# A new order of work on ScalarE, VectorE and GpSimd in the attention steps of a fused transformer block

## What is computed

```python
x = x + L0_xattn(layernorm(x), ctx)          # one head
x = x + L0_ffn(layernorm(x))                 # dense, with a routed low-rank part
# third block: 32 query heads, 8 key/value heads of 128
q = rmsnorm(heads(layernorm(x) @ q_proj.T), q_norm_w)
k = rmsnorm(heads(ctx @ k_proj.T), k_norm_w);  v = heads(ctx @ v_proj.T)
scores = q @ k.T / sqrt(128) + mask          # four query heads share one k and v
x = x + (softmax(scores) @ v) @ o_proj.T
x = x + down(silu(gate(n)) * up(n))          # n = layernorm(x), 4-bit weights
```

## Time and profile before

| | us |
|---|---|
| median of 3 runs (lowest, highest) | 960.37 (960.29, 961.23) |
| profiled execution: time | 960.64 |
| its span (first to last instruction) | 958.8 |
| outside the span | 1.8 |

### The profile page before, as it was taken

The page is one execution under the profiler, slowest core; times in us unless marked ns, Lnnn a source line. Parts: engine busy times, 40 slices in busy tenths (PEclk is TensorE's granted clock), DMA queues, the critical chain, the costliest instruction groups (busy, mean ns, idle before and its releaser), DMA issues.

```text
span 958.8 us, 14594 instructions
## 1 busy us (share of the span) xinstructions
PE 888.9 (93%) x4096; PEld 709.9 (74%) x4096; DVE 601.8 (63%) x1132; ACT 462.7 (48%) x1716; POOL 513.3 (54%) x559
## 2 busy tenths in 40 slices
PE   6999999979699999999999899999986899999996
PEld 5786887867487777777777777777765678888885
DVE  6316514323466666666666666666665579899887
ACT  4543740324455555555555555555563244443442
POOL 4333450322766666666666666666655246556562
PEclk9999999989899999999999999999997999999999
DMA  7401010112555555645555555565762224443312
GB/s 254 161 30 56 23 54 13 45 34 77 167 173 167 169 166 165 177 150 168 168 168 168 155 168 168 169 170 161 227 207 77 88 77 154 153 153 141 125 41 89
DMA packets 75249, 126.46 MB, mean 132 GB/s; under 512 B 8429, under 2 KB 46061, under 8 KB 75182
## 3 DMA queue, kind: packets, MB, share of 16 engines
q1 hardware_dynamic: 75182, 125.74, 42.0%
HBM read 90.06 MB, written 35.65 MB: 131 GB/s over the span
## 4 chain that ended last, share of the span: by engine, by line
PE 41%; DVE 23%; ACT 17%; issue 11%; POOL 5%; DMA 2%; ACTq 1%; DVEq 1%; SPq 0%; POOLq 0%
PE bank L1211 9%; PE bank L1212 8%; PE bank L1213 8%; ACT prob L765 7%; DVE bank L1053 6%; DVE split L1018 4%; DVE nmax L1059 4%; DVE tb L1045 4%; ACT headT L736 3%; ACT probT_hi L727 3%; PE bank L1379 3%; ACT aoT_hi L741 3%; PE bank L1380 3%; PE bank L1408 2%; PE bank L1409 2%
## 5 line engine op out<-in xcount | busy, mean ns | idle before, releaser
L765 ACT ACTIVATE prob<-bank,nmax 128x128 f32<-128x128 f32 x256 | 90.7, 366 | 84.2 <-DVE nmax L1059 84.2
L756 ACT ACTIVATE bank<-bank 128x128 f32<-128x128 f32 x256 | 67.9, 265 | 130.2 <-DVE tb L1040 130.2
L1211 PE MATMUL bank<-split,xnT_hi 128*128 128x512 f32 x288 | 115.6, 401 | 4.8 <-POOL split L464 4.8
L1212 PE MATMUL bank<-split,xnT_hi 128*128 128x512 f32 x288 | 113.3, 393 | 0.0
L1213 PE MATMUL bank<-split,xnT_lo 128*128 128x512 f32 x288 | 113.2, 393 | 0.0
L1211 PE MATMUL bank<-split,aoT_hi 128*128 128x512 f32 x256 | 103.0, 402 | 3.9 <-DVE aoT_lo L1032 3.9
L1032 DVE TENSOR_TENSOR aoT_lo<-bank,aoT_hi 128x512 fp32r<-128x512 f32 x64 | 44.3, 692 | 96.3 <-ACT aoT_hi L741 96.3
L1438 PEld LDWEIGHTS bank<-kv,headT 128*128 128x128 f32 x512 | 63.8, 195 | 52.5 <-issue 34.9
L1212 PE MATMUL bank<-split,aoT_hi 128*128 128x512 f32 x256 | 102.0, 398 | 0.0
L1213 PE MATMUL bank<-split,aoT_lo 128*128 128x512 f32 x256 | 101.9, 398 | 0.0
L1438 PE MATMUL bank<-kv,headT 128*128 (+1 forms) x512 | 75.0, 291 | 27.8 <-ACT headT L736 27.4
(11 more groups left out here) (151 smaller groups left out, 2210.2 us busy)
## 6 DMA issues: line engine op xcount, KB each, us to landing
block_bounce<-tb SPq DMA_DIRECT2D x244, 128.0 KB, 2.3
land<-block_bounce SPq DMA_DIRECT2D x61, 512.0 KB, 3.2
raw<-in_wqo_dram SPq DMA_DIRECT2D x62, 256.0 KB, 3.0
kv<-in_ffn_w_dram SPq DMA_DIRECT2D x14, 768.0 KB, 4.4
kv<-in_ffn_z_dram SPq DMA_DIRECT2D x14, 768.0 KB, 5.6
kv<-in_up_s_dram SPq DMA_DIRECT2D x14, 256.0 KB, 5.9
resid<-in_x_dram SPq DMA_DIRECT2D x2, 1024.0 KB, 8.8
kv<-in_ctx_dram SPq DMA_DIRECT2D x1, 2048.0 KB, 10.6
```

Of the source, the lines that this page charges most:

```text
L756: done = act.activation(bank[5][:, tile(h)], bank[i % 2][:, tile(h)], ACT.Square, accum_out=ssq[:, i % 2, h:h + 1])
L765: done = act.activation(prob[:, tile(h)], bank[2 + i % 2][:, tile(h)], ACT.Exp, bias=nmax[:, h:h + 1], accum_out=rsum[:, h:h + 1])
L1211: pe.matmul(dst, l_hi, r_hi, start=first, stop=False)
L1212: pe.matmul(dst, l_hi, r_lo, start=False, stop=False)
```

## The change

What moves, by engine, in `step(j)`:

- **ACT.** Before: probT_hi(j+1), headT(j+4), aoT_hi(j), squares(j+6), exponentials(j+4), vcur_hi(j+2). After: squares(j+5), weight_hi of chunk j+10, headT(j+5), aoT_hi(j+1), probT_hi(j+2), exponentials(j+4), vcur_hi(j+2).
- **DVE.** `weight_hi` leaves it. Before: add_out(j-1), rinv(j+3), aoT_lo(j), weight_hi, tb of queries j+6, tb of prob j+3, mask and maximum(j+4). After: rinv(j+3), add_out(j-1), tb of prob j+3, tb of queries j+6, mask and maximum(j+4), aoT_lo(j+1).
- **POOL.** Before: probT_lo(j+1), prob(j+3), weight_lo, rms(j+6), vcur_lo(j+2). After: prob(j+3), vcur_lo(j+1), rms(j+5), weight_lo, probT_lo(j+2).
- **Buffers.** `land` has two slots and `tb` one (before, the other way round). `bounce_read` now waits for copies one step older; the two transposes of a step wait for the bounce write of the step before.
- **SP.** A weight chunk is issued behind the bounce write of its step, not ahead of the read; chunks 4 to 9 come one step later (`EARLY_CHUNKS`), and so do their rounding and rest. Chunk 10 is issued in step 0 (before, step -1).
- **Start.** The first query weights are rounded one to three places earlier; `values(10)` is made ahead of Q(0), and V11 to V15 in steps -6 to -2, one a step.
- **End.** `ln_lo(3, 0..3)` on DVE and `ln_hi(3, 0..3)` on ACT move into step 61; the first gate product moves ahead of O(62).

```diff
-        tb = sb("tb", [P, 2, 2 * D])
-        land = sb("land", [P, 2 * D])
+        tb = sb("tb", [P, 2 * D])
+        land = sb("land", [P, 2, 2 * D])
...
-        VALUES_AT = {-6: (10, 11), -5: (12, 13), -4: (14,), -3: (15,)}
+        VALUES_AT = {-6: (11,), -5: (12,), -4: (13,), -3: (14,), -2: (15,)}
+        EARLY_CHUNKS = {-2: (4, 5), -1: (6, 7), 0: (8, 9)}
...
 # SP, bounce_read(c)
-                if c >= 1:
-                    sp.wait_ge(s_qt, min(c, STEPS))
-                if c >= PLAG + 1:
-                    sp.wait_ge(s_ptl, c - PLAG)
+                if c >= 2:
+                    sp.wait_ge(s_qt, min(c - 1, STEPS))
+                if c >= PLAG + 2:
+                    sp.wait_ge(s_ptl, c - PLAG - 1)
...
 # POOL, step(j)
+                if valid(j + 3):
+                    i = j + 3
+                    pool.wait_ge(s_ri, at(p, i) + 1)
+                    pool.tensor_tensor(heads(prob[:]), heads(prob[:]), over(rinv[:, 0:REP], P), ALU.mult)\
+                        .then_inc(s_pn, 1)
                 if valid(j + 1):
                     i = j + 1
...
+                    g = i // T if p is None else 2 * p + i // T
+                    pool.wait_ge(s_vh, at(p, i) + 1)
+                    pool.tensor_tensor(vcur_lo[:], val[:, bass.ds(g * P + (i % T) * NKV * P, P)], as32(vcur_hi[:]),
+                                       ALU.subtract).then_inc(s_vl, 1)
...
 # ACT, ahead of the steps
-            for m in range(T + 2):
+            for m in range(T + 3):
                 copy_values(m)
                 if 3 <= m:
                     ln_hi(2, m - 3)
-                if T <= m:
-                    hi(WGRP + m - T)
-            ln_hi(2, T - 1)
-            for c in range(WGRP + 2, WGRP + KT):
-                hi(c)
+                for c in ((WGRP, WGRP + 1), (WGRP + 2,), (WGRP + 3,))[m - T + 1] if T - 1 <= m < T + 2 else ():
+                    hi(c)
...
 # ACT, step(j), behind the squares and headT
+                if p is not None or 0 <= j < STEPS - 10:
+                    weight_hi(10 + j, p)
...
+                if valid(j + 1):
+                    act.wait_ge(s_e, at(p, j + 1) + 1)
+                    if p is not None or j >= 0:
+                        act.wait_ge(s_f, at(p, j + 1))
+                    act.activation(aoT_hi[:], bank[6][:], ACT.Copy).then_inc(s_ah, 1)
+                if valid(j + 2):
+                    i = j + 2
+                    act.wait_ge(s_br, 16 * (at(p, i) + PLAG + 1))
+                    if p is not None or i >= 1:
+                        act.wait_ge(s_e, at(p, i))
+                    act.activation(by_head(probT_hi[:]), landed(i + PLAG, 1), ACT.Copy).then_inc(s_pt, 1)
...
 # DVE, step(j)
+                if p is None and j == STEPS - 3:
+                    for t in range(HALF):
+                        ln_lo(3, t)
+                if valid(j + 1):
+                    dve.wait_ge(s_ah, at(p, j + 1) + 1)
+                    dve.tensor_tensor(aoT_lo[:], bank[6][:], as32(aoT_hi[:]), ALU.subtract).then_inc(s_al, 1)
```

More of the change, by code:

```diff
@@ L758, in step @@
                     done.then_inc(s_sq, 1)
+                for m in VALUES_AT.get(j, ()) if p is None else ():
+                    copy_values(m)
+                for n in EARLY_CHUNKS.get(j, ()) if p is None else ():
+                    weight_hi(n, None)
+                if p is not None or 0 <= j < STEPS - 10:
+                    weight_hi(10 + j, p)
+                if valid(j + LEAD - 1):
+                    i = j + LEAD - 1
+                    act.wait_ge(s_br, 16 * (at(p, i) + 1))
+                    if p is not None or i >= 1:
+                        act.wait_ge(s_c, at(p, i))
+                    act.activation(by_head(headT[:]), landed(i, 0), ACT.Copy).then_inc(s_qt, 1)
+                if p is None and j == STEPS - 3:
+                    for t in range(HALF):
+                        ln_hi(3, t)
+                if valid(j + 1):
[6 more added lines that the diff above has]
+                    act.wait_ge(s_br, 16 * (at(p, i) + PLAG + 1))
+                    if p is not None or i >= 1:
+                        act.wait_ge(s_e, at(p, i))
+                    act.activation(by_head(probT_hi[:]), landed(i + PLAG, 1), ACT.Copy).then_inc(s_pt, 1)
                 if valid(j + 4):
@@ L1029, in step @@
                     dve.reciprocal(rinv[:, 0:REP], rsum[:, 0:REP]).then_inc(s_ri, 1)
-                if valid(j):
-                    dve.wait_ge(s_ah, at(p, j) + 1)
-                    dve.tensor_tensor(aoT_lo[:], bank[6][:], as32(aoT_hi[:]), ALU.subtract).then_inc(s_al, 1)
-                if p is not None or 0 <= j < STEPS - 10:
-                    weight_hi(10 + j, p)
+                if valid(j - 1):
+                    add_out(j - 1, p)
+                if valid(j + 3):
+                    i = j + 3
+                    dve.wait_ge(s_pn, at(p, i) + 1)
+                    dve.wait_ge(s_bw, 16 * KT * (at(p, i) + PLAG))
+                    dve.transpose(blocks_of(1), split32(prob[:])).then_inc(s_tp, 1)
                 if valid(j + LEAD):
@@ L1114, in _ @@
                 if j == STEPS - 2:
-                    for t in range(HALF):
-                        ln_lo(3, t)
                     ln_aggr(3, HALF, HALF + 2)
@@ L1429, in step @@
                     done.then_inc(s_a, 1)
+                for m in VALUES_AT.get(j, ()) if p is None and j < -2 else ():
+                    values(m)
                 if valid(j + 4):
@@ L1458, in step @@
                     attend()
+                if p is None and j == STEPS - 2:
+                    pe.wait_ge(s_ex, STEPS)
+                    gate(0, None, 0)
                 if p is None and j == STEPS - 1:
```

136 lines of the change are left out of this document (44 added, 92 removed).

## The result

The changed kernel takes 986.35 us (median of 4 runs, 984.8 to 987.76) against 960.33 us for the kernel before (4 runs, 959.63 to 961.23): a ratio of 1.027, 95% interval 1.0252 to 1.0288. I had forecast 972, 962 to 982. The direction was right, the change is over twice as large as forecast (26.0 us for 11.7), and the time lies outside the range. The profiled execution has a span of 985.1 us.

A forecast was written before the change was run, and what follows sets the result against it. It took a ring through ACT and DVE, 7.85 us a step, to bound the kernel before, not PE. Stretch terms -14.3 + 4.6 + 10.8 + 4.8 + 6.0 = +11.9 on a median of 960.37 gave 972 us, range 962 to 982.

The forecast's parts named there:

- The ring of the loop: Each attention step: aoT_hi, probT_hi, exponentials, rinv, prob, vcur_lo, E, O wait in turn; 8.08 us, 0.22 longer than before.
- The rule that I weighed: Loop: frequent small PE idle times move the clock, losing more than the ring says; forecast kept the clock at 1.00.
- The loop's edges: Two back edges between O(4) and O(53): some 3.7 us together before, taken as unchanged; bounds 1.3 to 2.6 each.
- item 4: O(4) to O(53), before 388.8 us: 49 steps each 0.22 longer, +10.8.
- The start: Start to O(4): Q(0) at 204.5 as before, Q(0) to O(0) -14.3, O(0) to O(4) +4.6 us.
- Item 2: Q(0) to O(0), before 58.2 us: full clock and fewer waits give 43.9, so -14.3; bound -5.3.
- The two waits before E: Before O(0): E(0) and E(1) wait for exponentials, rinv, prob, vcur_lo; 2.8 us each.
- The stall in step 0: O(0) to O(4): ACT waits for weight chunk 10 until 253.4, headT behind it; +3 us.
- Items 5 and 6: O(53) to O(60): seven steps of 8.08 plus appended work, +4.8 us; O(60) to O(63): later O(61), +6, bounds +2 to +8.
- a rival at 6%: Loop: E and O at 1.2 GHz add some 3.2 us to one step in ten, +18, 990 us; chance 6%.
- O(63) to the end: After O(63): nothing changes.
- The range: Whole kernel: 962 to 982 us, from steps -7 to +7, end -4 to +2, start -3 to +9, edges -1 to +2.

The follow-up runs named there:

- experiments 1 and 2: Changed kernel with POOL's vcur_lo ahead of prob: 933.55 us; with that and ACT's vcur_hi ahead of the exponentials: 921.24 us.
- experiment 6: Changed kernel with weight chunk 10 rounded at the end of step 0 on ACT and POOL: 985.14 us.
- experiments but 4: 4 is the kernel before with only the rounding of weights (weight_hi) moved from DVE to ACT, ahead of the squares: 928.67 us.
- experiment 3: Changed kernel with three unread query products on PE in steps 58 to 60: 983.44 us.
- experiment 8: Experiment 5 with unread query products on PE in steps 58 to 61: 967.35 us.
- experiment 5: Changed kernel with the last steps' extra work moved: DVE's between the maximum and aoT_lo, POOL's ahead of probT_lo: 974.98 us.
- experiment 7: Changed kernel with vcur_hi and vcur_lo moved ahead, the last steps' extra work beside the ring, and chunk 10 rounded at the end of step 0: 904.8 us.
- experiment 11: Experiment 7 with the first two feed-forward units' transfers issued two each behind steps 53 to 55: 905.18 us.

## Why the forecast was right and wrong

**The ring of the loop: right.** I took 8.08 for a step of 8.10; its parts stand in the rows in the order given, and experiments 1 and 2 take it apart one member at a time (7.23, 7.03). The clock stayed at 1.00 over all 49 steps, with the wait of PE before each E. That it would was less sure than I wrote: I gave PE a gap of 0.8 us a step before, from 7.86 - 7.02, but the earlier trace rows have 18.7 us idle in 49 steps, 0.38 a step. The rule that I weighed, from the Trainium skill ("TensorE: Matmul & The Clock Gate", "A second HAM failure mode: psum-queue depth-cycling"), that frequent small idle times let the clock go up and down, is not borne out by this loop: one idle time of 0.84 in 8.10 us left it up.

**The loop's edges: mis-sized by 3.1.** I let the two edges cost what they cost before, some 3.7 together. They cost 0.6: the steps there are 8.41 and 8.35. DVE's late start fell into its wait for the exponentials entirely (rinv waits 1.31 instead of 1.23 there), not for a part of it. The 3.1 saved, less 1.0 for the 0.02 more a step, is the 2.1 by which item 4 came out shorter.

**The start: right in kind, 3.7 longer than forecast.** Q(0) to O(0) fell by 12.4 of the 14.3 forecast. Item 2 took Q(0) at full clock, since the wait ahead of it is short. The wait was 1.90 us, and PE in the changed kernel reads

```profile
204.79 0.50 PE L1203 MATMUL bank<-split,xnT_hi 128*128 128x512 f32 x1 [1.90 <-DVE xnT_lo L907]
...
205.83 0.39 PE L1204 MATMUL bank<-split,xnT_hi 128*128 128x512 f32 x1
206.06 0.58 PE L1205 MATMUL bank<-split,xnT_lo 128*128 128x512 f32 x1
...
242.03 0.47 PE L1203 MATMUL bank<-probT_hi,vcur_hi 128*128 128x512 f32 x1 [1.80 <-POOL vcur_lo L557]
249.77 0.47 PE L1203 MATMUL bank<-probT_hi,vcur_hi 128*128 128x512 f32 x1 [3.03 <-POOL vcur_lo L557]
```

It began at the high level and fell to the low one 1.3 us later, in the midst of work: Q(0) took 4.2 us instead of 2.7. But this was the luck of the profiled execution. In experiment 6, with the same code up to here and the same wait, PE reads

```profile
204.99 0.50 PE L1207 MATMUL bank<-split,xnT_hi 128*128 128x512 f32 x1 [1.90 <-DVE xnT_lo L911]
...
206.25 0.39 PE L1209 MATMUL bank<-split,xnT_lo 128*128 128x512 f32 x1
```

and Q(0) takes 2.9 us. Of the twelve profiles with the new start (the changed kernel and all experiments but 4), all with a wait of 1.90 us, Q(0) stayed at the high level in six and fell in six. Where it stayed, with nothing else changed up to O(0) (experiments 3, 6 and 8), Q(0) to O(0) took 44.2, 43.6 and 43.9 us, my 43.9; where it fell (the changed kernel and experiment 5), 45.8 and 45.3. So item 2 was right but for the clock, which it counted as certain. The two waits before E are 1.80 and 3.03 where I had placed 2.8 each. The stall in step 0 was forecast at 3 us, at its right place, ACT's rounding of chunk 10:

```profile
255.58 0.63 ACT L725 ACTIVATE split<-raw 128x512 fp32r<-128x512 f32 x1 [5.30 <-DMA raw<-in_wqo_dram]
```

It ended 2.2 us later than I had put it (253.4), but so did O(0), which began at 250.6 where I had 248.4; against O(0) the stall was as forecast. The first step was 11.83, not 11.2, and the next two 8.97 and 8.38, not 8.08. Experiment 6, which moves that instruction, has 36.0 us for O(0) to O(4), 1.2 to 2.5 less than the profiles without that edit; the rest of the excess is not taken apart.

**The last ten steps: this is the step that failed.** Items 5 and 6 said 90.1 us; it is 100.2. They took the whole stretch at full clock, and they priced the appended work at its length before. What the runs put in their place:

- *Work of DVE and POOL on the ring*, forecast at 4.8 + 6.0 = 10.8: experiment 5, which takes most of it away, gives 6.3 + 3.1 = 9.4. As a sum that was near; within it a term was far off. For step 57 I had 0.7 on DVE and the clock untouched. With stretch and clock together that step was 3.3 longer than one of the loop. I priced the subtractions by their rows before, about 0.68, and didn't ask what POOL does at that moment. The groups of DVE from 700 to 780 us, of the kernel before and then of the changed one:

```profile
L1080 DVE TENSOR_TENSOR split<-kv 128x512 fp32r<-128x512 int32 x4 | 2.7, 683 | 0.0
```

```profile
L1074 DVE TENSOR_TENSOR split<-kv 128x512 fp32r<-128x512 int32 x3 | 4.1, 1398 | 0.0
L1069 DVE TENSOR_TENSOR kv<-kv 128x512 f32<-128x512 int32 x2 | 3.6, 1778 | 0.0
```

  And two of them one behind the other in the changed kernel, with what POOL does (it is idle behind this):

```profile
736.89 1.76 DVE L1069 TENSOR_TENSOR kv<-kv 128x512 f32<-128x512 int32 x1
738.57 0.68 DVE L1074 TENSOR_TENSOR split<-kv 128x512 fp32r<-128x512 int32 x1
...
736.84 1.26 POOL L575 TENSOR_TENSOR probT_lo<-land,probT_hi 128x512 fp32r<-128x512 f32 x1 [6.67 <-ACT probT_hi L766]
```

  The same instructions take 0.68 when POOL has no such work, here, before and in experiment 5, and some 1.77 where a two-input subtraction or product of POOL (`probT_lo`, `up_scale`) runs at the same time. The rows look as if the two took turns: DVE ends 0.55 behind the end of POOL's instruction, here (738.65 and 738.10) as in step 57 (726.71 and 726.16), and there POOL's product, which began while DVE was at work, took 1.71 instead of 1.27. The Trainium skill ("GPSIMD Engine Reference", "Specifications") says that GpSimd contends with VectorE's instructions that have two SBUF inputs. The traces agree, with 0.68 against 1.77; no run here varied that alone, and how much of the 9.4 us it holds is not measured.
- *The clock*, forecast at nothing: filling PE in steps 58 to 61 gives another 5.3 + 1.5 = 6.8 us (experiment 8). I had this mechanism as a rival at 6%, and priced it nearly right (3.2 us a step at the low level; 2.8 measured), but put it in the loop, where PE waits 0.84. The place where it decides is where PE has no Q: there the same ring leaves it idle 3.56 us of a step, the 0.84 and the 2.72 of the missing product, and E and O, which are on the ring, then run at half speed for most of their length. I had row with 0.83 for O(60) to O(63) before and still took items 5 and 6 at full clock.
- *The rest.* With both removed the ten steps take 83.9, where the ring alone would give 8.1 x 10 = 81. The steps behind the unit loads (8.48 and 9.08 there) hold 1.4 of it.

These gains depend on the order in which they are taken: experiment 3 tried the filler alone, and it gave nothing that can be told from none. The work on the ring makes PE wait, and the wait brings the clock down; each hides part of the other. The sizes of both parts are differences of single profiles, in which the same code gave 69.7 and 72.1 us, so they are good to some 2 us; of the medians, experiment 5 takes 11.4 us off and experiment 8 another 7.6.

**O(63) to the end**, 2.4 longer, is open. Nothing of the change lies there, and the other profiles, with the same work in that stretch, had 196.1 to 199.0, so most of it may be the spread of single executions; no run was made to find out.

**The range.** Its bounds for the end of the attention were -4 to +2 in all, set around work of DVE and POOL. For these steps the clock was in no term's bounds (only item 2 has it), only in a rival that I put elsewhere.

## What to carry to other kernels

When an edit reorders work on several engines, follow the ring instruction by instruction from each engine's order: one swap of two GpSimd instructions was worth 53 us of 986 here, and a 0.5 us instruction standing behind a 1 us one was the bound of the whole loop. Then follow the same ring again in each stretch where the mix of work differs, above all where TensorE runs out of independent work, because there a serial ring can bring TensorE's clock down too (0.66 in experiment 5, though not with the shorter ring of experiment 7), and the matmuls on it lengthen it further. Work appended to a step costs nothing only at the place in the step where its engine waits. Look there also at what the other of VectorE and GpSimd does: here subtractions of 0.68 us took 1.77 beside a two-input instruction of GpSimd. And read a stretch from more than one profile where you can: the first product's clock differed between executions of the same code.

## What the runs showed of the hardware

- Unread matmuls kept the clock up and paid: the same steps took 10.6 us at a granted clock of 0.66 without them and 8.13 at 1.00 with them.
- The length of PE's wait alone does not tell the level. Behind waits of 3.56 us a step it was down for most of E and O (experiment 5); with 2.18 of 6.75 a step it stayed up (experiment 7); behind one of 2.41 it fell within the next product, at 661.4 us of experiment 11, and was up again by 664.9.
- The clock fell while PE was working, 1.3 us after a wait of 1.90 us, and stayed low to the end of Q(0) and into the product behind it; after the same wait it stayed up in six of twelve profiles.
- A subtraction of 128x512 on DVE took 1.77 instead of 0.68 us beside a two-input instruction on POOL. POOL's took its usual 1.26 when it had begun first, and 1.71 instead of 1.27 when DVE was already at work.
- A read of 512 KB landed 8.1 us after its issue among six weight transfers (experiment 7), and 3.3 us in the loop.
